# Adding self-attention's causal mask on VectorE instead of TensorE and ScalarE

## What is computed

```python
kv_c   = rms_norm(x @ wkv_down.T, kv_norm_w)          # latent of 128
q      = concat([q_nope, rope(q_pe)]);  k = concat([k_nope, rope(k_rope)])
scores = einsum('bqhd,bkhd->bhqk', q, k) * scale
causal = tril(ones((112, 112)))
scores = where(causal, scores, -inf)
out    = einsum('bhqk,bkhd->bqhd', softmax(scores), v) @ wo.T
```

## Time and profile before

| | before |
|---|---|
| median of 3 runs | 857.99 us (857.32 to 858.27) |
| the profiled execution, its own time | 858.94 us |
| span of its instructions | 857.1 us |
| TensorE busy | 827.0 us, 96% |
| VectorE busy | 518.0 us, 60% |
| ScalarE busy | 470.3 us, 55% |
| GpSimd busy | 241.7 us, 28% |
| granted TensorE clock | 0.996 of full speed |

### The profile page before, as it was taken

How to read it: one execution, slowest core, us unless ns; L and a number is a source line. 1 busy time by engine, 2 the same in 40 slices (tenths; PEclk the granted TensorE clock), 3 DMA queues, 4 the chain that set the end, 5 groups by cost and what they waited for, 6 DMA issues and landing times.

```text
span 857.1 us, 13364 instructions
## 1 busy us (share of the span) xinstructions
PE 827.0 (96%) x4302; PEld 706.4 (82%) x4302; DVE 518.0 (60%) x962; ACT 470.3 (55%) x1221; POOL 241.7 (28%) x284
## 2 busy tenths in 40 slices
PE   7999999999999999999998899999999999999997
PEld 5887887888788777888877689888888988889885
DVE  4755654753664548687787566355665655646466
ACT  6427545753843556977785526063755737647050
POOL 0142320230132031655654002602233322321420
PEclk9999999999999999999999999999999999999999
DMA  9113225315132406322120113624563655644422
GB/s 336 67 44 111 74 53 152 121 43 160 73 96 51 153 23 213 87 59 57 50 70 24 53 47 85 259 85 150 174 218 117 229 172 184 199 140 144 130 79 86
DMA packets 41597, 99.99 MB, mean 117 GB/s; under 512 B 15888, under 2 KB 23952, under 8 KB 39920
## 3 DMA queue, kind: packets, MB, share of 16 engines
q1 hardware_dynamic: 30496, 61.62, 23.0%
q0 software_dynamic: 11056, 37.79, 13.6%
HBM read 71.59 MB, written 20.97 MB: 108 GB/s over the span
## 4 chain that ended last, share of the span: by engine, by line
PE 77%; issue 9%; ACT 4%; DVE 4%; SPq 2%; DMA 2%; POOL 1%; POOLq 0%; ACTq 0%; DVEq 0%
PE ps L1545 61%; PE ps L1894 2%; PE ps L1566 2%; PE ps L1778 2%; SPq L556 2%; PE ps L1605 2%; PE ps L1884 1%; ACT Pt L885 1%; PE ps L1709 1%; PE ps L1597 1%; DMA stage<-in_wa 1%; PE ps L1896 1%; PE ps L1632 1%; PE ps L1560 1%; PE ps L1718 1%
## 5 line engine op out<-in xcount | busy, mean ns | idle before, releaser
L642 POOL TENSOR_TENSOR Pt<-Pt,rowinv 112x448 f32<-112x448 f32 x64 | 59.7, 933 | 188.2 <-DVE rowinv L1155 187.8
L1545 PE MATMUL ps<-x2T_hi,ws_hi 128*128 128x448 f32 x256 | 95.8, 374 | 3.7 <-ACT h_hi L1020 3.7
L885 ACT ACTIVATE Pt<-ps,negmax 112x112 f32<-112x112 f32 x256 | 87.1, 359 | 19.3 <-DVE negmax L1148 19.1
L1545 PE MATMUL ps<-x2T_hi,ws_lo 128*128 128x448 f32 x256 | 94.3, 368 | 0.0
L1545 PE MATMUL ps<-x2T_lo,ws_hi 128*128 128x448 f32 x256 | 94.2, 368 | 0.0
L1019 ACT ACTIVATE hf<-ps,b 128x448 f32<-128x448 f32 x64 | 40.5, 633 | 93.0 <-PE ps L1545 73.9
L1545 PE MATMUL ps<-w_hi,h_hi 128*128 128x512 f32 x224 | 89.9, 401 | 0.0
L1545 PE MATMUL ps<-w_hi,h_lo 128*128 128x512 f32 x224 | 88.4, 395 | 0.0
L1545 PE MATMUL ps<-w_lo,h_hi 128*128 128x512 f32 x224 | 88.4, 395 | 0.0
L1092 DVE TENSOR_TENSOR h_lo<-hf,h_hi 128x448 fp32r<-128x448 f32 x64 | 39.8, 623 | 47.0 <-ACT h_hi L1020 46.6
L1431 DVE TENSOR_TENSOR acc<-ps,acc 128x512 f32<-128x512 f32 x56 | 38.6, 689 | 45.0 <-PE ps L1545 38.1
(11 more groups left out here) (291 smaller groups left out, 2225.8 us busy)
## 6 DMA issues: line engine op xcount, KB each, us to landing
stage<-in_wf SPq DMA_DIRECT2D x30, 513.0 KB
rows_in<-in_zeros SPq DMA_DIRECT2D x30, 256.0 KB, 4.1
xs<-rows_in POOLq DMA_DIRECT2D x29, 256.0 KB, 4.3
rows_out<-yb POOLq DMA_DIRECT2D x29, 256.0 KB
stage<-in_wa SPq DMA_DIRECT2D x4, 1408.0 KB, 6.6
stage<-in_wb SPq DMA_DIRECT2D x4, 1280.0 KB, 5.6
qr<-ro_hi SPq DMA_DIRECT2D x64, 56.0 KB, 1.9
qr<-ro_lo SPq DMA_DIRECT2D x64, 56.0 KB, 1.9
```

Of the source, the lines that this page charges most:

```text
L642: nc.gpsimd.tensor_tensor(p, p, rowinv[0:S, b % 2, :].unsqueeze(2).broadcast_to([S, GH, S]), ALU.mult).then_inc(norm_done, 1)
L885: last = nc.scalar.activation(Pt[0:S, b % 2, h * S:(h + 1) * S], ps[0:S, b % 2, h * S:(h + 1) * S], ACT.Exp, bias=negmax[0:S, b % 2, h:h + 1],
L1545: ins = mm(dst, w, x, start=start and i == 0, stop=stop and i == len(ops) - 1, skip_group_check=not (start and stop))
```

## The change

The mask product of self-attention goes from TensorE; the first real matmul opens the accumulation. ScalarE's copy of the turned scores to `sT` goes too: VectorE writes `sT` as bank + mask, the fp32 mask `maskf` being repeated over the four heads. `maskf` therefore gets a place that lives through self-attention. The mask is stored turned, and cross-attention's mask product swaps its two operands to match. VectorE's list of the last group gets its missing `("G", 7)`, behind S5. GpSimd gets one more wait in the loop of cross-attention: before it splits the key and value weights of the next group, the present group's V must be out of its bank.

```diff
@@ ATT_LAST_DVE
-    ("Z", 3), ("T", 4), ("S", 5), ("N", 5), ("Z", 4), ("S", 6), ("W", 2), ("N", 6), ("T", 5), ("W", 3), ("S", 7),
+    ("Z", 3), ("T", 4), ("S", 5), ("G", 7), ("N", 5), ("Z", 4), ("S", 6), ("W", 2), ("N", 6), ("T", 5), ("W", 3), ("S", 7),
@@ build
         maskb = sb("maskb", [P, S], BF16, at=both)
+        maskf = sb("maskf", [P, S], at=both)
...
-        maskf = sb("maskf", [P, S], at=first)
@@ GpSimd, split_lk
                 if isinstance(g, int):
                     pool.wait_ge(a_free["B"], NG * GH)
+                else:
+                    pool.wait_ge(x_free["V"], XJ.count(("V", 1), g - 1))
@@ ScalarE, att_step
-                elif kind == "G":
-                    act.wait_ge(job_done, at.number + 1)
-                    copy(sT[0:S, j % 2, :], ps[0:S, 6 + at.bank, 0:GH * S]).then_inc(a_free["G"], 1)
@@ VectorE, att_step
+                elif kind == "G":
+                    dve.wait_ge(job_done, at.number + 1)
+                    nc.vector.tensor_tensor(sT[0:S, j % 2, :].rearrange("p (h s) -> p h s", h=GH),
+                                            ps[0:S, 6 + at.bank, 0:GH * S].rearrange("p (h s) -> p h s", h=GH),
+                                            maskf[0:S, :].unsqueeze(1).broadcast_to([S, GH, S]), ALU.add)\
+                        .then_inc(a_free["G"], 1)
@@ TensorE, att_step, kind G
-                    mask(bank[0:S, 0:GH * S], maskb, identb)
...
-                        ins = mm(heads(bank[0:S, 0:GH * S]), w, x, start=False, stop=i == len(ops) - 1,
-                                 skip_group_check=True)
+                        ins = mm(heads(bank[0:S, 0:GH * S]), w, x, start=i == 0, stop=i == len(ops) - 1)
@@ TensorE, x_step, kind S
-                    mask(ps[0:S, j % 2, 0:GH * S], identb, maskb)
+                    mask(ps[0:S, j % 2, 0:GH * S], maskb, identb)
@@ layouts
-    o["mask"] = np.where(np.arange(P)[:, None] < np.arange(S), f(-3.0e38), f(0))
+    o["mask"] = np.where(np.arange(P)[:, None] > np.arange(S), f(-3.0e38), f(0))
```

## The result

The changed kernel takes 865.07 us in the median of 4 runs (864.36 to 867.22), the kernel before 857.65 beside it (857.07 to 858.27): a ratio of 1.0091, with a 95% interval of 1.0070 to 1.0111. It is 7.4 us slower. The forecast was 863.6 in a range of 860.5 to 867.2.

What follows compares the result with a forecast made beforehand. TensorE sets the time wherever it may start; additions late in VectorE's in-order list hold its gates. Groups add 1.13 + 2 x 1.64 + 1.22 = 5.6 us to the median of 857.99: 863.6, range 860.5 to 867.2.

Steps and rivals of the forecast that it cites:

- What is taken away and added: Per mask 0.19 us off TensorE, per copy some 0.43 off ScalarE (counted as nothing), per addition 0.61 onto VectorE.
- Step A: Gate at G2, every group: G1's addition queues behind N0 and SB1 on VectorE, so its bank comes free 1.46 us later.
- Step B: Gate at B1, which needs G2's bank from VectorE: S1 starts 1.57 us late, the chain behind it moves by 1.58.
- Step C: Steps 2 and 3: VectorE's fill becomes G3, SA0, G4, so S3's maximum comes 1.74 us late.
- E0: Next group's TensorE matmuls that need G5's bank: to start 21.7 us behind S0 instead of 19.45.
- Step D: Gate at the next group's E0: G5's addition stands behind N3, E0 starts 2.21 us late, holding all earlier delays.
- The masks behind the gate: Of 32 masks 11 pay back, 2.1 us; 21 lie in front of a gate and don't; a middle group saves 0.57.
- The sum: First group 1.13 us more, two middle groups 1.64 each, last 1.22: 5.6 us more.
- VectorE's burst: VectorE's work SA1, SA2, E0, O0 up to S4's maximum, behind E0's gate: starts 1.3 us late, less late than TensorE.
- Not slower: Rival: VectorE is idle 40%, G1's addition starts when its scores are there, all masks pay 6.1 us: 851.9; chance 0.08.
- Given back: Rival: G2 starts 1.46 us late, but the slip shrinks before E0 and most masks pay: within 1.7 us of 858; chance 0.09.
- More: Rival: VectorE's burst from SA1 to S4 becomes the bound, each group pays another 1 us or more: 868 and above; chance 0.08.

Runs made afterwards that it cites:

- e2: The kernel before without self-attention's mask product, ScalarE's copy left as it was (attention no longer causal): 856.34 us, ratio to before 0.9982.
- e9: Changed kernel with VectorE's additions reordered, G2 in front of Q21 on TensorE too, and the mask product back on TensorE: 856.36 us, ratio to before 0.9979.
- e4_g5: Changed kernel with only G5 moved in front of N3 in the loop's VectorE list: 862.32 us, ratio to before 1.0048.
- e1: Changed kernel with the additions G1, G2, G3 and G5 earlier in VectorE's list, no other engine's list touched: 854.84 us, ratio to before 0.9958.
- e8: e1 with a second VectorE instruction of the same size in front of each addition, result unused: 859.27 us, ratio to before 1.0014.
- e6: e1 with SA0 behind S3's maximum and G5 in front of Z1 on VectorE, in the loop's groups: 854.33 us, ratio to before 0.9949.
- e10: The kernel before, masks and copies where they were, only step 0's order changed in all engines' lists: 860.27 us, ratio to before 1.0025.
- e3: Changed kernel with the mask product back on TensorE, the mask halved in both places: 866.84 us, ratio to before 1.0092.
- e5: Changed kernel with only G1 moved in front of N0 and G2 in front of SB2 on VectorE, all groups: 859.29 us, ratio to before 1.0016.

## Why the prediction was right, step by step

- **What is taken away and added.** 0.613 us for the addition against 0.61. Cross-attention's swapped mask product costs 360 ns as before. Behind self-attention nothing moved by more than 0.3 us.
- **Step A.** G2's first matmul 5.80 us behind S0's transposes, forecast 5.9. The wait grew from 0.73 to 2.41: 1.46 for the later bank and 0.19 for the mask that no longer fills the gap, 2.38 in all.
- **Step B.** S1 8.80 us behind S0 instead of 7.37, 1.43 later; forecast 1.57.
- **Step C.** The order of the fill on VectorE is the forecast one, but its lengths are not:

```profile
159.23 0.18 DVE L1154 RECIPROCAL rowinv<-rowsum 112x4 f32<-112x4 f32 x1 [0.18 <-ACT Pt L887]
159.33 0.62 DVE L1256 TENSOR_TENSOR sT<-ps,maskf 112x448 f32<-112x448 f32 x1
159.96 1.27 DVE L1091 TENSOR_TENSOR wa_lo<-stage,wa_hi 128x768 fp32r<-128x768 f32 x1
```

  SA0's split takes 1.27 us instead of the 0.96 assumed, and its successor starts 1.20 later instead of 0.87. Against that stand step B, taken 0.14 too long, and the reciprocals N2 and N3, behind which the addition starts after 0.10 us instead of 0.26. S3's maximum comes 18.62 us behind S0 (forecast 18.52). That the gate at E0 lies within 0.1 us of its place is luck in so far as these errors cancel.
- **Step D.** E0 21.61 us behind S0, forecast 21.7. In the first group 22.21 against 20.56 before, 1.65 later (forecast 1.70). In the last, W0 21.76 against 20.46, 1.30 later (forecast 1.60).
- **The masks behind the gate** pay and the others don't: e2 gives 1.6 us for all masks where the prediction has 2.1, and 0.58 for a middle group where it has 0.57. This holds for the order of before: in e9's order masks in front of a gate do pay, since what opens the gate stands behind them.
- **The sum.** The four groups take 2.56, 3.16, 3.13 and 0.94 us more than before, 9.8. With 1.54 for each of the three falls taken out it is 1.02, 1.62, 1.59 and 0.94: 5.2 where the prediction had 1.13, 1.64, 1.64 and 1.22, 5.6. Self-attention itself began 1.1 us earlier in this execution, behind the first loads, which the change doesn't touch.

What the sum lacked is a term of its own: **the falls of the clock**. 7.4 us measured less 5.2 to 5.4 (the sum above, and the estimate of 863.0) leaves some 2.0 to 2.2, for about one and a half falls in an execution. The prediction asked of a longer wait only what it delays, and not what TensorE does behind it. That 865.07 lies in the stated range is therefore part luck: the upper end made room for slower additions and for a longer burst on VectorE, neither of which is what filled it, and the slowest run, 867.22, lies on that end.

Two of the prediction's own signs show the missing term. A middle group was to last 73.9 us and lasts 75.4 in the profiled execution (73.9 with 1.54 taken out). And VectorE's burst ends 3.0 us behind its old place (S4's maximum 28.21 us behind S0 instead of 25.19), where more than 1.5 was named as a sign of being wrong. It begins 1.39 us late, forecast 1.3; behind that VectorE idles 0.40 and 1.03 us for matmuls of E0 and O0 that run at the lower clock. In e4_g5, whose second group has no fall, it ends 1.40 late.

**The rivals.** *Not slower* fails by its own row: N0 at 146.01 is in front of G1's addition at 148.20. e1 is the kernel that meets its condition, and 854.8 is what it brings; 851.9 was too good, since masks in front of a gate stay free. The Trainium skill (PSUM — Partial Sum Buffer, "Engine vs sequencer instructions") has VectorE's queue first in, first out; the trace agrees, since e1 takes G1's scores 1.61 us behind S0 and the changed kernel 5.13, with 2.3 us of waiting in front. *Given back* fails: middle groups are 1.6 us longer without the falls. *More* had a further 1 us or more a group, and in the profiled execution three groups do pay 1.5 more; but its cause, VectorE's burst as the bound, fails: e8 adds 17 us to VectorE and stays 5.8 us under the changed kernel.

**Open.** What decides whether the clock falls behind a given wait. In the profiled executions every fall in self-attention stands behind a wait of 1.88 us or more; there are nine falls for fifteen such waits. Before, e1, e2 and e6 to e10, whose waits there are 1.7 us at most, have none, nor has e3 behind its 1.70. But G2's wait of 2.41 us has a fall behind it in e4 and none in the changed kernel, and e5 has one behind one of its three waits of 1.88. Nor do the wait and the work around it decide by themselves: in e4 the same wait of 2.41 us stands in front of the same G2 at 147, 220 and 294 us, and the first has no fall behind it. And the four runs of e3 are one program, with mean clocks of 0.990, 0.994, 0.994 and 0.996. No run separates the length of a wait from what TensorE did around it, nor either from the moment at which the wait falls.

## What to carry to other kernels

Moving work to an idler engine is a change of two queues: look up the place of the instruction in the receiver's list, count what waits in front of it there, and see who waits for it. Busy shares (60% here) don't answer this; the same instructions cost 7 us in one place of VectorE's list and gained 3 in another. Work saved in front of a gate (a place where an engine waits for another) pays only as far as what opens the gate itself stands behind that work, and a TensorE wait made longer can cost more than its length, by the clock behind it.

## What the runs showed of the hardware

- A wait of 1.9 to 2.4 us between stretches of full work can be followed by 3.3 us at 1.2 GHz, which costs 1.5 us: granted clock 0.66 in a stretch of 5 us with TensorE busy throughout. The Trainium skill (TensorE: Matmul & The Clock Gate, "HAM oscillation — how this bites in real kernels") has the same pattern, of waits in a loop that bring the lower level back again and again; here the waits are shorter than those it tells of, and nine of fifteen did it, not each.
- A subtraction on VectorE with both inputs in SBUF, 128 x 768 (SA0's split), takes 0.95 us alone (e6) and 1.40 where GpSimd's multiplication runs beside it; in e1 that one is this row:

```profile
155.23 0.93 POOL L650 TENSOR_TENSOR Pt<-Pt,rowinv 112x448 f32<-112x448 f32 x1 [3.12 <-DVE rowinv L1162]
```

It ends at 156.16, 0.59 us behind the subtraction's start, and the subtraction takes 0.45 us longer. In the changed kernel the two are together for 0.46 us, and it takes 0.32 longer (1.27). The Trainium skill (SBUF — State Buffer, "Who interferes with whom") says that such an instruction and one of GpSimd that reads SBUF exclude each other; the row agrees, roughly.
